# Keeping the attention scores in SBUF between the two passes of a softmax over batches

## The reference, cut to what matters

```python
# q = layernorm(x), k = v = ctx_1024, each (64, 128, 256)
score = jnp.einsum('bci,bcj->bij', k, q) / math.sqrt(l)     # (64, 256, 256)
score = jax.nn.softmax(score, axis=0)                       # over the batches
out = jnp.einsum('bci,bij->bcj', v, score)
x = x + out
# then x = x + moe(layernorm(x)): router, top 2 of 8 experts, 256 -> 512 -> 256
```

## Time and profile before

| | |
|---|---|
| time, median of 3 runs | 856.29 us |
| times of the runs | 856.29, 869.16, 856.03 us |
| span of the profiled execution | 909.8 us (the page gives no other time of it) |
| busy share of the span | PE 85%, DVE 68%, POOL 63%, ACT 43% |
| mean granted clock of PE | 0.927 |
| HBM | 156 GB/s over the span |

### The profile page before, as it was taken

The page is one execution under the profiler, slowest core; times in us unless marked ns, Lnnn a source line. Parts: engine busy times, 40 slices in busy tenths (PEclk is TensorE's granted clock), DMA queues, the critical chain, the costliest instruction groups (busy, mean ns, idle before and its releaser), DMA issues. The chain is left out here.

```text
span 909.8 us, 22499 instructions
## 1 busy us (share of the span) xinstructions
PE 770.1 (85%) x5931; PEld 649.5 (71%) x5932; DVE 622.8 (68%) x1520; ACT 390.1 (43%) x715; POOL 574.0 (63%) x815
## 2 busy tenths in 40 slices
PE   6999996999996449888989887989588889879886
PEld 5678885878885338766877776978367778767775
DVE  6998999899998758655655654363465656556554
ACT  3555664576666204333333433143133333334331
POOL 5664776788884056666576566366766666665663
PEclk9999997999997559999999999799789999999998
DMA  7887773488885124444344443343533343333330
GB/s 227 251 250 240 237 228 114 137 269 266 267 275 192 53 60 134 131 147 157 118 148 156 142 133 119 112 140 76 159 106 111 106 129 108 97 115 116 96 107 2
DMA packets 82200, 137.20 MB, mean 151 GB/s; under 512 B 10075, under 2 KB 55140, under 8 KB 82032
## 3 DMA queue, kind: packets, MB, share of 16 engines
q0 software_dynamic: 23104, 68.43, 24.9%
q1 hardware_dynamic: 59056, 68.26, 23.9%
HBM read 94.56 MB, written 47.59 MB: 156 GB/s over the span
## 5 line engine op out<-in xcount | busy, mean ns | idle before, releaser
L680 PE MATMUL psum<-work,w1T_high 128*128 128x256 f16 x1248 | 227.4, 285 | 53.5 <-ACT work L1067 36.6
L1059 ACT ACTIVATE work<-psum,slots 128x256 f32<-128x256 f32 x312 | 130.2, 471 | 309.4 <-PE psum L680 233.0
L703 PE MATMUL psum<-w2T_high,slots 128*128 x1248 | 214.7, 277 | 6.2 <-issue 5.1
L680 PEld LDWEIGHTS psum<-work,w1T_high 128*128 x1248 | 124.0, 102 | 85.9 <-issue 67.2
L680 PE MATMUL psum<-work,w1T_low 128*128 128x256 f16 x624 | 177.6, 285 | 3.5 <-issue 3.5
L703 PE MATMUL psum<-w2T_low,slots 128*128 x624 | 172.4, 276 | 1.7 <-issue 1.7
L952 DVE CAST slots<-work 128x512 f16<-128x512 f32 x156 | 71.0, 455 | 138.4 <-ACT work L1059 114.8
L703 PEld LDWEIGHTS psum<-w2T_high,slots 128*128 128x128 f16 x1248 | 119.6, 99 | 23.2 <-issue 9.2
L561 PE MATMUL psum<-slots,work 128*128 (+1 forms) x512 | 124.0, 392 | 7.4 <-ACT slots L991 6.8
L540 POOL DMA_INDIRECT rows_second<-slots x78 | 82.3, 1055 | 66.0 <-issue 35.6
L968 DVE SCALAR_TENSOR_TENSOR slots<-psum,slots 128x256 f32<-128x256 f32 x156 | 68.2, 478 | 78.5 <-remote 63.9
(11 more groups left out here) (126 smaller groups left out, 1125.2 us busy)
## 6 DMA issues: line engine op xcount, KB each, us to landing
work<-in_ctx SPq DMA_DIRECT2D x96, 256.0 KB, 3.5
rows_first<-slots SPq DMA_DIRECT2D x32, 514.0 KB, 3.9
slots<-in_x SPq DMA_DIRECT2D x32, 256.0 KB, 3.8
work<-in_L_ffn_w SPq DMA_DIRECT2D x32, 256.0 KB, 3.2
work<-in_x SPq DMA_DIRECT2D x32, 256.0 KB, 3.1
slots<-rows_first,slots POOLq DMA_INDIRECT x86
rows_second<-slots POOLq DMA_INDIRECT x78
slots<-rows_second,slots POOLq DMA_INDIRECT x78
```

The lines of the kernel that those rows point to most:

```text
L680: mm = pe.matmul(h, w1T[pw][:, f, c, bass.ds(e * P, P)], xT[r2][:, (px * HC + c) * GROUP:(px * HC + c + 1) * GROUP], start=(c == 0 and px ...
L703: mm = pe.matmul(y, act16[r2][pa][:, f * GROUP + s * P:f * GROUP + (s + 1) * P], w2T[pw][:, f, bass.ds(e * DIM, DIM)], start=(f == 0 and p ...
L1059: last = act.activation(act32[r2][:, f * GROUP:(f + 1) * GROUP], psum[:, 2 + 2 * r2 + f // 2, (f % 2) * GROUP:(f % 2 + 1) * GROUP], ACT.Ge ...
```

## The change

In the first pass ACT copies each pair's scores from PSUM into the pair's slot (after the queries have been used, two steps behind the queries), and DVE's maximum reads the slot and waits for the copy (`m_kept`) instead of for the scores. PE's banks come free with the copy. In the second pass the scores are no longer computed and the context is no longer loaded: DVE subtracts the maximum from the slot in place. DVE's share of the sum goes: POOL adds the odd batches (512 columns per pair), and PE adds the even ones by multiplying them with the identity into one PSUM bank that accumulates over all pairs (`add_even`). DVE adds the two sums at the end.

```diff
--- before
+++ after
@@ -154,8 +153,8 @@
         w1T = [sb(f"w1T_{p}", [P, FC, HC, EXPERTS * P], F16) for p in ("high", "low")]
         w2T = [sb(f"w2T_{p}", [P, FC, EXPERTS * DIM], F16) for p in ("high", "low")]
         smax = sb("smax", [P, 3, 2 * DIM])
-        sums = smax[:, 1:3, :]
-        ssum = sums[:, 0, :]
+        ssum = smax[:, 1, :]
+        odd_sum = smax[:, 2, :]
         choice = smax[:, 0, 0:ROUNDS * BATCH].rearrange("p (r b) -> p r b", r=ROUNDS)
         work = sb("work", [P, 18, DIM])
         ctx_ring = work[:, 0:8, :]
@@ -371,7 +371,10 @@
 
         L_CTX = 2
         L_MAX = 3
-        L_SUM, L_LOW = 2, 2
+        L_COPY = 2
+        L_ADD = 1
+        SUM_BANK = 3
+        L_LOW = 2
         L_CT, L_PV, L_XN, L_LOWX, L_XNT, L_LG, L_P = 1, 2, 4, 5, 5, 6, 7
         L_XL, L_STORE = 1, 8
 
@@ -396,24 +399,22 @@
 
             sp.wait_ge(s_setT, 1)
 
-            def load_exps(i, k, n):
-                m, r = i + k, k % RING
-                sp.wait_ge(m_score, m + PAIRS - RING + 1)
-                sp.dma_start(ctx_ring[:, 2 * r:2 * r + 2, :], pair_of(ctx, m * 2)).then_inc(m_ctx_in[r], 16)
+            def load_weights(i, k, n):
+                m = i + k
                 if k % 2 == 0:
 
                     j = (k // 2) % 2
                     after(sp, e_wT, n * 2 + k // 2 - 1)
                     sp.dma_start(stage[:, 4 * j:4 * j + 2, :], w1_rows[bass.ds(m * P, 2 * P), :].rearrange("(q p) h -> p q h", p=P)).then_inc(e_w_in[j], 16)
                     sp.dma_start(stage[:, 4 * j + 2:4 * j + 4, :].rearrange("p a b -> p (a b)"), w2_rows[bass.ds(m * (P // 2), P), :]).then_inc(e_w_in[j], 16)
-            pipeline(sp, PAIRS, RING, RING, 0, load_exps)
+            pipeline(sp, PAIRS, RING, RING, 0, load_weights)
 
             def attend(i, k, n):
                 if live(i, k, 0, PAIRS):
                     m, r = i + k, k % RING
                     if isinstance(i, int) and i + k < RING:
 
-                        sp.wait_ge(m_score, 2 * PAIRS)
+                        sp.wait_ge(m_score, PAIRS)
                         sp.wait_ge(e_wT, PAIRS // 2)
                     after(sp, a_ctxTp, m - 1)
                     sp.dma_start(a_ctx[:, 2 * (k % 2):2 * (k % 2) + 2, :], pair_of(ctx, m * 2)).then_inc(a_ctx_in[k % 2], 16)
@@ -474,12 +475,13 @@
             def add_up(i, k, n):
                 m = i + k
                 pool.wait_ge(e_exp, m + 1)
+                odd = slot(m * 2 + 1, 0, 2 * DIM)
                 if isinstance(m, int) and m == 0:
                     pool.wait_ge(m_top, 1)
-                    pool.tensor_copy(sums[:, :, SUM_DVE:], slot2(0, SUM_DVE, 2 * DIM - SUM_DVE)).then_inc(e_sump, 1)
+                    pool.tensor_copy(odd_sum, odd).then_inc(e_sump, 1)
                 else:
                     pool.wait_ge(e_sump, m)
-                    pool.tensor_tensor(sums[:, :, SUM_DVE:], slot2(m * 2, SUM_DVE, 2 * DIM - SUM_DVE), sums[:, :, SUM_DVE:], ALU.add).then_inc(e_sump, 1)
+                    pool.tensor_tensor(odd_sum, odd, odd_sum, ALU.add).then_inc(e_sump, 1)
             pipeline(pool, PAIRS, RING, RING, 0, add_up)
 
             pool.wait_ge(e_recip, 1)
@@ -565,21 +567,14 @@
             def scores_max(i, k, n):
                 m, r = i + k, k % RING
                 pe.wait_ge(m_ctx_in[r], landed_at(i, k, RING))
-                after(pe, m_max, m - 1)
+                after(pe, m_kept, m - 1)
                 for j in range(2):
                     pe.wait_ge(m_q, m * 2 + j + 1)
                     score(m * 2 + j, 2 * (k % 2) + j, 2 * r + j, j == 1)
             pipeline(pe, PAIRS, RING, RING, 0, scores_max)
 
-            def scores_exp(i, k, n):
-                m, r = i + k, k % RING
-                pe.wait_ge(m_ctx_in[r], landed_at(i, k, RING) + 16 * (PAIRS // RING))
-                if isinstance(i, int) and i == 0 and k < 2:
-                    pe.wait_ge(m_max, PAIRS - 1 + k)
-                after(pe, e_diff, m - 1)
-                for j in range(2):
-                    score(m * 2 + j, 2 * (k % 2) + j, 2 * r + j, j == 1)
-                if k % 2 == 0:
+            def add_even(i, k, n):
+                if k % 2 == 0 and live(i, k, 0, PAIRS):
                     j = (k // 2) % 2
                     pe.wait_ge(e_w_in[j], n * 32 + 32 * (k // 4) + 32)
                     if isinstance(i, int) and i == 0 and k == 0:
@@ -591,12 +586,20 @@
                     for f in range(FC):
                         mm = pe.transpose(psum[:, 5 + 2 * j, f * P:(f + 1) * P], stage[:, 4 * j + 2 + f // 2, (f % 2) * P:(f % 2 + 1) * P], ident[:])
                     mm.then_inc(e_wT, 1)
-            pipeline(pe, PAIRS, RING, RING, 0, scores_exp)
+                if live(i, k, L_ADD, PAIRS):
+                    m = i + k - L_ADD
+                    if isinstance(m, int) and m == 0:
+                        pe.wait_ge(m_kept, PAIRS)
+                    pe.wait_ge(e_exp, m + 1)
+                    mm = pe.matmul(psum[:, SUM_BANK, :], ident[:], slot(m * 2, 0, 2 * DIM), start=isinstance(m, int) and m == 0,
+                                   stop=isinstance(m, int) and m == PAIRS - 1)
+                    if isinstance(m, int) and m == PAIRS - 1:
+                        mm.then_inc(e_even, 1)
+            pipeline(pe, PAIRS, RING, RING, L_ADD, add_even)
 
 
             def attend(i, k, n):
                 if isinstance(i, int) and i == 0 and k == 0:
-                    pe.wait_ge(e_diff, PAIRS)
                     pe.wait_ge(e_wlow, PAIRS // 2)
                 if live(i, k, L_CT, PAIRS):
                     m, r = i + k - L_CT, (k - L_CT) % 2
@@ -722,14 +725,14 @@
                     for j in range(2):
                         dve.bn_stats(stats[:, r, j, :], slot(m * 2 + j, 0, DIM)).then_inc(m_stat, 1)
                 if live(i, k, L_MAX, PAIRS):
-                    m, r2 = i + k - L_MAX, (k - L_MAX) % 2
-                    dve.wait_ge(m_score, m + 1)
-                    banks = psum[:, 2 * r2:2 * r2 + 2, :]
+                    m = i + k - L_MAX
+                    dve.wait_ge(m_kept, m + 1)
+                    kept = slot2(m * 2, 0, 2 * DIM)
                     if isinstance(m, int) and m == 0:
-                        dve.tensor_copy(smax[:, 0:2, :], banks).then_inc(m_max, 1)
+                        dve.tensor_copy(smax[:, 0:2, :], kept).then_inc(m_max, 1)
                     else:
                         dve.wait_ge(m_max, m)
-                        dve.tensor_tensor(smax[:, 0:2, :], banks, smax[:, 0:2, :], ALU.max).then_inc(m_max, 1)
+                        dve.tensor_tensor(smax[:, 0:2, :], kept, smax[:, 0:2, :], ALU.max).then_inc(m_max, 1)
                 if live(i, k, 0, PAIRS):
                     m, r = i + k, k % RING
                     wait_apart(dve, m_stat, m * 2 + 2)
@@ -742,18 +745,11 @@
             dve.wait_ge(m_top, 1)
 
             def exponentials(i, k, n):
-                if live(i, k, L_SUM, PAIRS):
-                    m = i + k - L_SUM
-                    dve.wait_ge(e_exp, m + 1)
+                if live(i, k, 0, PAIRS):
+                    m = i + k
                     if isinstance(m, int) and m == 0:
-                        dve.tensor_copy(sums[:, :, 0:SUM_DVE], slot2(0, 0, SUM_DVE)).then_inc(e_sumv, 1)
-                    else:
-                        dve.wait_ge(e_sumv, m)
-                        dve.tensor_tensor(sums[:, :, 0:SUM_DVE], slot2(m * 2, 0, SUM_DVE), sums[:, :, 0:SUM_DVE], ALU.add).then_inc(e_sumv, 1)
-                if live(i, k, 0, PAIRS):
-                    m, r2 = i + k, k % 2
-                    dve.wait_ge(m_score, m + PAIRS + 1)
-                    dve.tensor_tensor(slot2(m * 2, 0, 2 * DIM), psum[:, 2 * r2:2 * r2 + 2, :],
+                        dve.wait_ge(m_kept, PAIRS)
+                    dve.tensor_tensor(slot2(m * 2, 0, 2 * DIM), slot2(m * 2, 0, 2 * DIM),
                                       smax[:, 0:1, :].to_broadcast([P, 2, 2 * DIM]), ALU.subtract).then_inc(e_diff, 1)
                 if k % 2 == 0 and live(i, k, L_LOW, PAIRS):
 
@@ -765,9 +761,9 @@
                     last = dve.scalar_tensor_tensor(w2_at(w2T[1]), w2_bank, WSCALE, w2_at(w2T[0]), ALU.mult, ALU.subtract)
                     last.then_inc(e_wlow, 1)
             pipeline(dve, PAIRS, RING, RING, L_LOW, exponentials)
-            dve.wait_ge(e_sumv, PAIRS)
+            dve.wait_ge(e_even, 1)
             dve.wait_ge(e_sump, PAIRS)
-            dve.tensor_tensor(ssum, ssum, sums[:, 1, :], ALU.add).then_inc(e_total, 1)
+            dve.tensor_tensor(ssum, psum[:, SUM_BANK, :], odd_sum, ALU.add).then_inc(e_total, 1)
             dve.wait_ge(e_total, 1)
 
             dve.reciprocal(ssum[:, 0:PROD_POOL], ssum[:, 0:PROD_POOL]).then_inc(e_recip, 1)
@@ -985,12 +981,17 @@
         @block.scalar
         def _(act):
             def queries(i, k, n):
-                m, r = i + k, k % RING
-                act.wait_ge(m_norm, m + 1)
-                for j in range(2):
+                if live(i, k, L_COPY, PAIRS):
```

(13 more changed lines are left out.)

## The result

The changed kernel takes 890.91 us (median of 4 runs, 888.12 to 896.24) against 856.16 us: a ratio of 1.0371, with a 95% interval from 1.0298 to 1.0444. (One run of the kernel before took 869.16 us; the two medians alone give 1.041.) Run again later it took 890.59 against 860.84 us, 1.0346 (1.0312 to 1.0379), with 3.23 us per pair in the first pass, where 3.1 to 3.2 was expected of this second run, and 2.14 in the second. It is slower, by some 3.5%; 886 us were forecast.

A forecast was written before the change was run, and what follows sets the result against it. VectorE, busy nearly all of both passes, bounds them now; after the change a two-pair loop lengthened by exclusion bounds the first. First pass +32.8, second -3, carried to the median: 856.3 + 29.8 = 886 us, range 866 to 900.

The forecast's parts named there:

- The loop over two pairs: First pass: ScalarE's copy ahead of the waiting maximum closes a loop of 5.53 us per two pairs, 2.76 per pair.
- The exclusion in the first pass: Maximum with two SBUF inputs and GpSimd's normalisation cannot overlap: power 0.89 us later in one loop of two, 3.21 per pair.
- Rival (a): First pass: small GpSimd operations do not collide with the maximum; +20 us there, 873 us in all; chance 0.16.
- The ends of the first pass: First copies start the chain some 2.6 us later; last maxima end about as much sooner; set against each other.
- The second pass: Differences and GpSimd's adds hold each other up: 2.22 us per pair against 2.27; with two waits gone, -3 us.
- Rival (b): Differences and adds overlap fully, no exclusion: first pass loses 20 us, second gains 18; 858 us; chance 0.08.
- the 0.1: First pass: by the skill's rule the tiny GpSimd operation before the power holds the maximum back 0.1 us; 1.4 us more.
- Costed at nothing: Second pass: removing TensorE's second scores and the second context load saves nothing, since VectorE is the full engine there.
- Rival (c): TensorE falls to 1.2 GHz; second pass takes 2.7 us per pair instead of 2.22: +15, 901 us; chance 0.09.
- Rival (d): Normalisation has unseen slack, first pass keeps 2.04 us per pair: 853 us, or 838 without exclusion in second; chance 0.05.
- The sum: Whole kernel: 909.8 + 32.8 - 3 = 939.6 us on the profiled execution; carried to the median, 856.3 + 29.8 = 886.
- the 53.5 us: Gap between the profiled span, 909.8 us, and the median run, 856.29; taken as untouched by the change.

## Why the prediction was right, point by point

**The loop over two pairs** is shown: opening it by the lag or by the order of VectorE's body takes 17 to 21 us away, with every operation still there. Its price was 5.53 us per two pairs; freed of the exclusion it measured 5.44 away from the ends of the pass. The copy was sized at 1.06 and takes 1.00, which is most of the difference.

**The exclusion in the first pass** is shown by the running maximum in PSUM: one operand's place changes, the power goes back to 0.71, and the step to 2.67, from 3.14 in the changed kernel and from 3.06 at the same grant. The power was said to be late by 0.89 in one loop of two; its record of 1.60 instead of 0.71 is that figure. Where the grant is held at 1.00, one power in two is late and two pairs take 6.27 to 6.36 where 6.42 was forecast. In the changed kernel only 9 powers of 32 are, and the waits for scores, longer at the lower clock and not in the forecast, seem to make up for the others; that the mean of the 28 steps, 3.22, meets the forecast's 3.21 is in part luck.

Rival (a), no collision on GpSimd, had a step of 2.75; the kernel whose maximum was freed is close to it, 2.67 and 1.018 x 856.3 = 872 us against the rival's 873. Its steps are unequal too, from 1.9 to 2.5 and from 2.9 to 3.6 in turn, so it is the power's record and not the inequality of the steps that tells rival (a) from the forecast.

**The ends of the first pass** were set against each other. The first maximum came 0.9 us later, not 2.6, and the last two steps saved 0.3; the last maximum starts 33.9 us later than in the first profile of the kernel before (109.3 against 75.4), where 32.8 was forecast.

**The second pass** gained 3.9 us between first and last difference and 0.8 between there and the products, 4.7 where 3 was forecast. The term that was off is the step: 2.22 was worked out, 2.14 measured, 2.18 once the alternation has set in. The add of 512 columns was sized at 1.18 and takes 1.09, and so it holds VectorE for 0.95 instead of 1.03; the first differences run before any add. Rival (b), no exclusion, is refuted by the lengthened adds and differences, and the kernel with the final maximum in PSUM shows what it would have been worth: 1.73 per pair, as worked out from VectorE alone.

The Trainium skill's rule, page "SBUF — State Buffer", section "Who interferes with whom", that of two such operations the later one waits out the earlier, agrees with the trace in both passes (in the second, holds of 1.08 and 0.95 us in turn). What no row of the kernel before showed, an operand of two columns, is now shown from one side: the power waits out a 1024-wide maximum, 1.60 instead of 0.71. From the other side it does not show: the maximum at 43.27 starts inside the two-column operation of 43.16 to 43.38 and still takes 1.23, and no maximum of the changed kernel takes more than 1.227, so the 0.1 that would have made 887 us of the forecast did not appear.

**Costed at nothing**: the removed scores and loads. In this the forecast was right: in the second pass VectorE waits for nothing, and without exclusion that pass runs at VectorE's rate. TensorE's sum stayed hidden, with TensorE busy 14.99 of 20 us:

```profile
120.00:140.00 20.00, 14.99 (x61) 7.45 (x60) 20.00 (x20) 14.60 (x20) 15.96 (x10) 1.00 0.45 143
```

**Rival (c), the clock**, came where it was only mentioned, in the first pass, and not as a loss of 15 us: 2.4 to 5.3 us at most. In the second pass, for which it was priced, the grant is 1.00 once the pass is under way (the line above). Its sum was off too: 2.8 us at double length are 5.6 per two pairs, not 5.4, so 2.8 per pair and +18. **Rival (d)**, slack in the normalisation, did not appear.

**The sum**: +29.8 forecast; the products start 29.9 later, the profiled spans differ by 28.5, the medians by 34.75 at first and 29.8 when run again. Counted in the first profiles, the first pass lost 1.1 us more than forecast and the second gained 1.7 more; that these nearly cancel is luck. The assumption that the 53.5 us between the first profile's span and the median lie behind the two passes was right as well: both profiles of the kernel before show the same passes, and 754.5 against 703.9 us behind them.

What the change set out for was there to be had. VectorE's work in the second pass did shrink to 1.73, and the copy did fit beside the queries, but the order of VectorE's body and the place of two operands took back more than both.

## What to carry to other kernels

When an operation is put between two others of a software pipeline, follow the loop through every engine's program order and count the steps it spans: here one more in-order hand-over turned a loop over three pairs into one over two, which no busy share showed, and raising one lag undid it. When data moves from PSUM to SBUF, look at what the other operand of each VectorE operation is and at what GpSimd reads at that time; leaving one operand in PSUM cost VectorE nothing here.

## What the runs showed of the hardware that was not expected

A VectorE operation with one operand in SBUF and the other, and its output, in PSUM takes no longer than the same with all three in SBUF: 1.217 to 1.229 us against 1.225 for the 1024-wide maximum. And a two-column operation on GpSimd suffers as much from a long VectorE operation as a wide one: the power grew from 0.71 to as much as 1.73, by more than it takes.
